# A four-layer decoder in one kernel: weights loaded in earlier stages, first steps without the weight preparation, output stored tile by tile, and a causal bias added in place

## The chip, the cores and the metric

The kernel runs on one core of one Trainium2 chip. A core has TensorE (PE), VectorE (DVE), ScalarE (ACT), GpSimd (POOL) and SyncE (SP), the last of which here only issues DMAs. The metric is the time of one execution in microseconds on the device, as the median of several runs.

## What is computed

A decoder of four layers over 128 sequences of 64 tokens with 128 features, all in float32. Each layer is an attention, a cross-attention to a second sequence `ctx_1024` and a feed-forward part, each followed by residual and LayerNorm:

```python
x = _layernorm(x + _L0_attn_ref(x, ...))               # 16 heads of 8, causal
x = _layernorm(x + _L0_xattn_ref(x, ctx, ctx, ...))    # 16 heads of 8
x = _layernorm(x + _L0_ffn_ref(x, ...))                # weights and tokens quantised
x = _layernorm(x + _L1_attn_ref(x, ...))               # linear attention
x = _layernorm(x + _L1_xattn_ref(x, ctx, ctx, mask, ...))
x = _layernorm(x + _L1_ffn_ref(x, ...))                # 8 experts, gated, routed
x = _layernorm(x + _L2_attn_ref(x, ...))               # recurrent, 4 inner layers
x = _layernorm(x + _L2_xattn_ref(x, ctx, ctx, lenS2, ...))
x = _layernorm(x + _L2_ffn_ref(x, ...))                # 8 experts, top 2
x = _layernorm(x + _L3_attn_ref(x, ...))               # 16 heads, relative bias
x = _layernorm(x + _L3_xattn_ref(x, ctx, ...))         # 8 heads of 64, own and ctx keys
x = _layernorm(x + _L3_ffn_ref(x, ...))                # 16 slots: gather, experts, combine
```

The softmax of the causal attention is what the last part of the change touches: scores of 64 queries by 64 keys per head plus a bias (0 or a large negative number), row maximum, subtract, exp.

## The kernel before

`x` and `ctx` stay in SBUF for the whole run, features on partitions: 128 x 8192. Twelve stages follow one another, each a function that opens a `Scope` with its own SBUF tiles, all of PSUM and its own semaphores, and a block with one program per engine. When a scope closes, its semaphores are cleared and all engines meet at a barrier (L42 to L45); the next stage then starts with its own DMAs on SP. A stage's first steps wait for all of its loads, then prepare its weights: DVE takes the mean of the output weight's rows out of it (so that LayerNorm's mean need not be subtracted later), PE multiplies it by the value bias into one output bias, DVE copies that to SBUF, and PE waits for it (`bo_ready`) before its first projection. The last stage is followed by a block in which SP stores `x` in four DMAs of 1 MB (L3386 to L3391).

Within a stage each engine's order is written out by `staggered(turns, period, (place, step), ...)` (L145): all steps of all tiles are sorted by tile times period plus place, and issued in that order; semaphores do the rest.

`mha` (L190) is used by four stages: causal (L0_attn), plain (L0_xattn), masked (L1_xattn) and relative (L3_attn). It has 32 tiles of 256 tokens. Per tile PE projects K and Q ("QK", L341, L342) and V (L349), computes scores in two halves of two PSUM banks each (S0, S1, L363), transposes the exponentials (T0, T1, L376), forms sums and outputs (ZO, L391, L398), projects out (y, L406, L408) and takes the variance (L413). Six of the eight PSUM banks form three pairs that go round: one serves S1(t), T0(t), S1(t+1); one QK and T1; one S0(t), V(t+1), S0(t+1). `wait_emptied` makes PE wait until the former user of a pair has been read (`emptied`). With a bias, DVE adds it to the scores from PSUM into the SBUF tile E (`add_bias`, L529), takes the row maximum (L550) and subtracts it (L560) within E; without a bias both read PSUM. Bank pairs of scores are thus free after the add with a bias, and after the subtract without. ACT takes exp, and DVE normalises (L569) and closes the tile (L583: scale and residual). The places of each variant stand in the table `PLACES`.

`quantised_ffn` (L0_ffn) first quantises its weights (ACT L765, DVE up to L869), and only then does PE turn the first tokens (L677), which DVE (L890) quantises. `linear_attention` (L1_attn, PE L1007, DVE L1147), `padded_attention` (L2_xattn, DVE L2344), `joint_attention` (L3_xattn, DVE L2648, PE L2497) and `slot_combine` (DVE L3281) begin alike. `routed_experts` (L1_ffn, L2_ffn) begins with a load of the router and DVE's copy of the identity beside it (L1517). It ends with 16 groups of 512 tokens: DVE and ACT weigh and mix the experts' rows (L1666, L1495), PE sums them with the residual (`gather_sum`, L1410, L1411), ACT squares (L1500), PE takes the variance (L1418), ACT forms the inverse root (L1506, L1508), DVE closes (L1672). The last stage's tiles are closed at L3333.

## Time and profile before

| | us |
|---|---|
| time, median of 3 runs | 4991.06 (4987.13 to 4992.86) |
| time of the profiled execution | 4995.66 |
| its span in the trace | 4993.9 |
| PE busy | 4483.5 (90%) |
| DVE busy | 3497.6 (70%) |
| ACT busy | 3088.7 (62%) |
| POOL busy | 1543.2 (31%) |

| stage | from | to |
|---|---|---|
| L0_attn (causal) | 5.8 | 334.6 |
| L0_xattn (plain) | 335.6 | 630.7 |
| L0_ffn | 631.7 | 942.7 |
| L1_attn | 943.6 | 1137 |
| L1_xattn (masked) | 1138 | 1445 |
| L1_ffn | 1446 | 1966 |
| L2_attn | 1967.8 | 3110 |
| L2_xattn | 3111.3 | 3191 |
| L2_ffn | 3192 | 3730.6 |
| L3_attn (relative) | 3731.7 | 4037.3 |
| L3_xattn | 4038.3 | 4633 |
| L3_ffn, last part (combine) | 4824.6 | 4980.3 |
| store | 4981.6 | 4993 |

The page divides the span into 40 slices, one digit of tenths per slice. The span is that of the instructions; the time of the execution is 1.8 us longer. The granted clock of PE is 0.955 of full speed over the span. The page:

```
PE   8989968798978997999999999679979989999887
DVE  8977767466865335989995999653349966666747
PEclk9999989898989998999999999889989999999989
DMA  2000000000021113000000000301130000000110
```

### The profile page before, as it was taken

The page shows a single profiled execution, that of the slowest core. Times are in us where ns is not written, and L with a number is a line of the kernel's source. Part 1 is how long each engine was busy: PE and PEld are TensorE (multiplying, and loading weights), DVE is VectorE, ACT ScalarE, POOL GpSimd, SP SyncE. Part 2 cuts the span into 40 slices and gives each one's busy share as a digit, 9 for nine tenths or more (in the row PEclk, how much of TensorE's full clock was granted, in tenths as well). Part 3 has the DMA queues.
Part 4 walks back from the last instruction along what each step waited for, and adds up shares of the span by engine and source line. Part 5 has one row for each costly group of instructions (what it writes and reads, how often), then busy time and mean ns, then how long its engine had stood idle before and what let it go on. Part 6 is the DMA issues. An engine that isn't in the chain of part 4 may idle for free. (4 is left out here: it accounts for less than half of the span.)

```text
span 4993.9 us, 101269 instructions
## 1 busy us (share of the span) xinstructions
PE 4483.5 (90%) x37623; PEld 2954.1 (59%) x37623; DVE 3497.6 (70%) x5384; ACT 3088.7 (62%) x5449; POOL 1543.2 (31%) x1948
## 2 busy tenths in 40 slices
PE   8989968798978997999999999679979989999887
PEld 6767746565757774444444443466656757777664
DVE  8977767466865335989999995653349966666747
ACT  5766667475665334888888887652247844444355
POOL 4434434213424771000000000037726622222326
PEclk9999989898989998999999999889989999999989
DMA  2000000000021113000000000301130000000110
GB/s 82 2 4 2 2 5 1 4 1 12 2 70 33 52 52 113 1 1 1 1 1 1 1 1 6 118 26 52 53 90 2 2 14 2 1 2 2 55 54 35
DMA packets 122746, 119.54 MB, mean 24 GB/s; under 512 B 19360, under 2 KB 104353, under 8 KB 120993
## 3 DMA queue, kind: packets, MB, share of 16 engines
q1 hardware_dynamic: 104864, 77.38, 5.0%
q0 software_dynamic: 17408, 35.69, 2.5%
q8 instruction: 317, 5.19, 0.4%
q14 instruction: 157, 1.28, 0.1%
HBM read 82.60 MB, written 30.41 MB: 23 GB/s over the span
## 5 line engine op out<-in xcount | busy, mean ns | idle before, releaser
L2242 POOL TENSOR_TENSOR L_xattn_E<-L_xattn_E,L_xattn_rz 128x256 f32<-128x256 f32 x16 | 10.2, 637 | 1276.7 <-DVE L_xattn_rz L2397 1276.7
L1335 POOL DMA_INDIRECT L_ffn_xg<-L_ffn_xrows,L_ffn_take x272 | 264.0, 971 | 317.5 <-DVE L_ffn_take L1619 235.3
L1395 PEld LDWEIGHTS L_ffn_ps<-L_ffn_down,L_ffn_mT 128*128 128x128 f32 x1904 | 247.5, 191 | 105.6 <-issue 79.3
L1341 POOL DMA_INDIRECT L_ffn_yrows<-L_ffn_yo,L_ffn_put x272 | 269.1, 989 | 94.5 <-issue 58.5
L1377 PE MATMUL L_ffn_ps<-L_ffn_up,L_ffn_xT 128*128 x544 | 258.6, 557 | 21.2 <-issue 9.2
L2483 POOL TENSOR_TENSOR L_xattn_E<-L_xattn_E,L_xattn_rz 128x1024 f32<-128x1024 f32 x64 | 123.9, 1935 | 477.8 <-DVE L_xattn_rz L2701 477.8
L1395 PE MATMUL L_ffn_ps<-L_ffn_down,L_ffn_mT 128*128 x1904 | 259.4, 276 | 2.5 <-DVE L_ffn_yo L1641 1.3
L1802 PE MATMUL L_attn_ps<-L_attn_mix,L_attn_wck 128*128 128x512 f32 x512 | 240.6, 592 | 0.0
L1818 PE MATMUL L_attn_ps<-L_attn_rl,L_attn_wcv 128*128 128x512 f32 x512 | 240.6, 592 | 0.0
L1478 ACT ACTIVATE L_ffn_mT<-L_ffn_ps 128x512 f32<-128x512 f32 x136 | 81.2, 597 | 237.9 <-PE L_ffn_ps L1386 237.9
L1630 DVE TENSOR_TENSOR L_ffn_m<-L_ffn_b,L_ffn_ps 128x512 f32<-128x512 f32 x136 | 93.6, 688 | 185.1 <-PE L_ffn_ps L1377 185.1
L301 POOL TENSOR_TENSOR L_attn_Kbd<-L_attn_Kt,main_head_of_row 128x1024 f32<-128x1024 f32 x64 | 147.9, 2311 | 242.7 <-issue 225.0
L1626 DVE TENSOR_TENSOR L_ffn_m<-L_ffn_sg,L_ffn_ps 128x352 f32<-128x352 f32 x136 | 70.9, 522 | 213.3 <-ACT L_ffn_sg L1468 213.3
L301 POOL TENSOR_TENSOR L_xattn_Kbd<-L_xattn_Kt,main_head_of_row 128x1024 f32<-128x1024 f32 x64 | 121.2, 1894 | 298.9 <-issue 277.3
L560 DVE TENSOR_TENSOR L_attn_E<-L_attn_E,L_attn_mx 128x1024 f32<-128x1024 f32 x128 | 210.8, 1647 | 2.3
L550 DVE TENSOR_REDUCE L_xattn_mx<-L_xattn_ps 128x16 f32<-128x1024 f32 x128 | 155.8, 1218 | 62.5 <-PE L_xattn_ps L363 62.3
L660 POOL TENSOR_SCALAR L_ffn_aq<-L_ffn_aq,L_ffn_qinv 128x512 f32<-128x512 f32 x64 | 127.0, 1999 | 171.5 <-ACT L_ffn_aq L808 171.5
L529 DVE TENSOR_TENSOR L_attn_E<-L_attn_ps,L_attn_bias 128x512 f32<-128x512 f32 x256 | 164.0, 681 | 22.8 <-PE L_attn_ps L363 19.6
L319 POOL COPY L_attn_Vz<-L_attn_Vt 64x64 f32<-64x64 f32 x512 | 168.3, 329 | 37.0 <-ACT L_attn_Vt L461 7.7
L1818 PEld LDWEIGHTS L_attn_ps<-L_attn_rl,L_attn_wcv 128*128 128x128 f32 x512 | 97.3, 190 | 122.5 <-issue 122.5
L1802 PEld LDWEIGHTS L_attn_ps<-L_attn_mix,L_attn_wck 128*128 128x128 f32 x512 | 92.6, 190 | 127.1 <-issue 92.8
L468 ACT ACTIVATE L_attn_E<-L_attn_E 128x1024 f32<-128x1024 f32 x128 | 134.8, 1053 | 47.8 <-DVE L_attn_E L560 47.7
(607 smaller groups left out, 13302.1 us busy)
## 6 DMA issues: line engine op xcount, KB each, us to landing
L_ffn_row_hot<-L_ffn_yrows SPq DMA_DIRECT2D x32, 256.0 KB, 2.9
L_ffn_col_hot<-L_ffn_yrows SPq DMA_DIRECT2D x32, 256.0 KB, 3.3
L_ffn_w<-in_L_ffn_e_W SPq DMA_DIRECT2D x32, 256.0 KB, 4.5
L_ffn_xrows<-L_ffn_xtok SPq DMA_DIRECT2D x42, 192.0 KB, 2.1
L_ffn_xg<-L_ffn_xrows,L_ffn_take POOLq DMA_INDIRECT x272, 2.5
L_ffn_yrows<-L_ffn_yo,L_ffn_put POOLq DMA_INDIRECT x272, 2.3
main_x<-in_xT SPq DMA_DIRECT2D x8, 512.0 KB, 7.6
main_ctx<-in_ctxT SPq DMA_DIRECT2D x4, 1024.0 KB, 11.5
```

The costliest lines, as they stand in the source:

```text
L301: pool.tensor_tensor(Kbd[u][:], Kt[u][:].rearrange("p (b o k) -> p b o k", b=NB, o=1).to_broadcast([P, NB, 4, S]), k["head_of_row"][:].rea ...
L319: z = pool.tensor_copy(Vz[u][64 * side:64 * side + 64, hp, b2:NB:2, :, c:c + 8], v[:, :, :, c:c + 8])
L468: act.activation(e, e, ACT.Exp).then_inc(exp_ready[half], 1)
L529: b = dve.tensor_tensor(E[t % 2][:, 8 * at:8 * at + 8, :].rearrange("p (a h) k -> p a (h k)", a=2), pair(f"S{half}", t)[:, g, :].rearrange ...
L550: dve.tensor_reduce(mx[t % 2][:, 16 * half:16 * half + 16], score_rows(half, t), AX, ALU.max) \
L560: dve.tensor_tensor(E[u][:, rows, :], score_rows(half, t), mx[u][:, rows].rearrange("p (a o) -> p a o", o=1).to_broadcast([P, 16, S]), ALU ...
L1335: pool.indirect_dma_start(xg[t % RING][:], None, xrows, bass.IndirectOffsetOnAxis(ap=take[:, t:t + 1], axis=0)) \
L1341: pool.indirect_dma_start(yrows, bass.IndirectOffsetOnAxis(ap=put[:, t:t + 1], axis=0), yo[t % RING][:], None).then_inc(scattered[t % RING ...
L1377: g = pe.matmul(ps[u][:, 0, 0:F], xT[u][:], up[:, bass.ds(at, F)], start=True, stop=True)
L1395: g = pe.matmul(ps[1][:, 3, 0:P], mT[u][0:rows[a], a * P:(a + 1) * P], down[0:rows[a], bass.ds(at + a * P, P)], start=(a == 0), stop=(a == ...
L1802: r = pe.matmul(ps[:, 5 + a % 2, :], wck[:, at(m)[0], a * P:(a + 1) * P], mix[:], start=True, stop=True)
L1818: r = pe.matmul(ps[:, 7, :], wcv[:, at(m)[0], a, :], rl[:, a, :], start=(a == 0), stop=(a == FT - 1))
```

## The change

**Weights early.** A new class `Early` holds tiles, one semaphore and their sources. The tiles of the next stages are allocated in an outer scope, and SP loads them in an earlier stage: those of L0_xattn, L0_ffn, L1_attn and L1_xattn (with its mask of 1 MB) in the first stage, behind x, the constants and ctx; those of L2_xattn in L2_attn; of L3_attn in L2_ffn; of L3_xattn (six of 256 KB) in L3_attn; of combine in the slots' expert stage. The routers are loaded in the first stage into tiles of the main scope, and DVE copies them. The lengths are laid out on 128 partitions on the host. Each `Early` is a scope, so eight further clears with barriers stand behind L1_xattn (four), L2_xattn (one), L3_xattn (two) and at the end (one).

```diff
+class Early:
+    def __init__(self, nc, ctx, name, **parts):
+        s = Scope(nc, ctx, name)
+        self.tile = {n: s.sb(n, shape, dt) for n, (shape, dt, _) in parts.items()}
+        self.source = {n: source for n, (_, _, source) in parts.items()}
+        self.loaded = s.sem("loaded")
+
+    def load(self, sp):
+        for n, source in self.source.items():
+            sp.dma_start(self.tile[n][:], source).then_inc(self.loaded, 16)
+
+    def wait(self, eng):
+        eng.wait_ge(self.loaded, 16 * len(self.tile))
...
                 for q, piece_loaded in enumerate(x_loaded):
                     c = slice(q * T // X_PIECES, (q + 1) * T // X_PIECES)
                     sp.dma_start(xres[:, c], d["xT"][:, c]).then_inc(piece_loaded, 16)
+                    if q == 0:
+                        sp.dma_start(bias_sb[:], bias).then_inc(bias_loaded, 16)
...
+                sp.wait_ge(rest_loaded, 16 * (len(LATER) + 4 + len(ROUTERS) + 1))
+            for stage in ahead:
+                stage.load(sp)
```

**First steps.** PE no longer waits for the prepared output weight or the output bias before its first tile. In `mha` the two bias products move to the first `outputs`, and DVE's copy to the first `normalise`:

```diff
-            pe.wait_ge(loaded, 16 * n_loads)
-            pe.wait_ge(weights, 1)
-            if has_wo:
-                pe.matmul(ps[:, 7, 0:1], W[3][:], column("bv"), start=True, stop=False)
-                pe.matmul(ps[:, 7, 0:1], k["center"][:], b_in[:], start=False, stop=True).then_inc(bo_mm, 1)
...
-            pe.wait_ge(bo_ready, 1)
+            wait_weights(pe)
+
+            def output_bias():
+                to = ps[:, 7, CT:CT + 1]
+                if has_wo:
+                    pe.wait_ge(weights, 1)
+                    pe.matmul(to, W[3][:], column("bv"), start=True, stop=False)
+                    pe.matmul(to, k["center"][:], b_in[:], start=False, stop=True).then_inc(bo_mm, 1)
...
             def outputs(t):
                 u = t % 2
+                if t == 0:
+                    output_bias()
...
             def normalise(t):
+                if t == 0:
+                    dve.wait_ge(bo_mm, 1)
+                    dve.tensor_copy(bo[:], ps[:, 7, CT:CT + 1]).then_inc(bo_ready, 1)
+                    dve.wait_ge(bo_ready, 1)
```

In `quantised_ffn` PE turns the first tokens, and DVE takes their range, before the weights are quantised; `w_ready` is waited for at the first expansion. In `linear_attention`, `padded_attention` and `joint_attention` the waits for the prepared weight move to the first `project_out`, while the one or two small bias products of PE stay in front.

PE's order at the head of L0_xattn, before (L330 and L331 are the bias products, L341 the K projection):

```order
L325 UNCONDITIONAL_BRANCH
L330 MATMUL L0_xattn_ps<-main_cols,L0_xattn_w3 128x1
L331 MATMUL L0_xattn_ps<-L0_xattn_b_in,main_center 128x1
L341 MATMUL L0_xattn_ps<-main_ctx,L0_xattn_w1 128x256
L342 MATMUL L0_xattn_ps<-main_x,L0_xattn_w0 128x256
```

and now (L375 is the K projection):

```order
L357 UNCONDITIONAL_BRANCH
L375 MATMUL L0_xattn_ps<-main_ctx,L0_xattn_early_w1 128x256
L376 MATMUL L0_xattn_ps<-main_x,L0_xattn_early_w0 128x256
L383 MATMUL L0_xattn_ps<-L0_xattn_early_w2,main_ctx 128x128 x2
L397 MATMUL L0_xattn_ps<-L0_xattn_Kbd0,L0_xattn_Qt0 64x256 x16
```

The two bias products have left the head; they come with the first `outputs`.

**The store.** The last block is gone. In `slot_combine` SP stores `x` in 16 pieces of 256 KB, each when its tile is closed:

```diff
+            for q in range(OUT_PIECES):
+                c = slice(q * T // OUT_PIECES, (q + 1) * T // OUT_PIECES)
+                sp.wait_ge(closed, (q + 1) * NT // OUT_PIECES)
+                sp.dma_start(out[:, c], k["x"][:, c]).then_inc(stored, 16)
+            sp.wait_ge(stored, 16 * OUT_PIECES)
...
-                for q in range(4):
-                    c4 = slice(q * T // 4, (q + 1) * T // 4)
-                    sp.dma_start(out[:, c4], k["x"][:, c4]).then_inc(stored, 16)
-                sp.wait_ge(stored, 64)
```

**The causal stage.** With `in_place=True` the bias is added to the scores where they lie in PSUM; maximum and subtract read PSUM, and the pair of banks is free after the subtract. The add no longer waits for the transposes of two tiles before. The places are new, the period of 9.2 is not:

```diff
-        scored = biased if bias is not None else sub_ready
+        scored = biased if bias is not None and not in_place else sub_ready
...
                     dve.wait_ge(s_mm[half], t + 1)
-                    if t >= 2:
+                    if t == 0:
+                        dve.wait_ge(bias_loaded, 16)
+                    if t >= 2 and not in_place:
                         dve.wait_ge(t_mm[half], t - 1)
...
+                        scores = pair(f"S{half}", t)[:, g, :].rearrange("p (a c) -> p a c", a=2)
                         b = dve.tensor_tensor(
-                            E[t % 2][:, 8 * at:8 * at + 8, :].rearrange("p (a h) k -> p a (h k)", a=2),
-                            pair(f"S{half}", t)[:, g, :].rearrange("p (a c) -> p a c", a=2),
+                            scores if in_place else E[t % 2][:, 8 * at:8 * at + 8, :].rearrange("p (a h) k -> p a (h k)", a=2),
+                            scores,
...
-            "QK": 0.0, "V": 1.0, "S0": 2.9, "bias0": 5.6, "max0": 9.5, "sub0": 9.6, "exp0": 11.6, "T0": 11.2,
...
+            "QK": 0.4, "V": 2.8, "S0": 3.6, "bias0": 4.3, "max0": 8.3, "sub0": 9.3, "exp0": 9.9, "T0": 13.6,
```

DVE's order for one tile in the causal stage, before (L529 add, L550 maximum, L560 subtract, L569 normalise, L583 close; two adds per half; the scope of this stage is L0_attn):

```order
L569 TENSOR_TENSOR L0_attn_On1<-L0_attn_ps,L0_attn_rz1 128x256 [waits L0_attn_y_mm,L0_attn_rz_ready]
L529 TENSOR_TENSOR L0_attn_E1<-L0_attn_ps,L0_attn_bias 128x512 [waits L0_attn_t_mm0,L0_attn_s_mm0]
L529 TENSOR_TENSOR L0_attn_E1<-L0_attn_ps,L0_attn_bias 128x512
L550 TENSOR_REDUCE L0_attn_mx1<-L0_attn_E1 128x16 [waits L0_attn_sub_ready0,L0_attn_biased0]
L560 TENSOR_TENSOR L0_attn_E1<-L0_attn_E1,L0_attn_mx1 128x1024 [waits L0_attn_t_mm0,L0_attn_max_ready0]
L529 TENSOR_TENSOR L0_attn_E1<-L0_attn_ps,L0_attn_bias 128x512 [waits L0_attn_t_mm1,L0_attn_s_mm1]
L529 TENSOR_TENSOR L0_attn_E1<-L0_attn_ps,L0_attn_bias 128x512
L550 TENSOR_REDUCE L0_attn_mx1<-L0_attn_E1 128x16 [waits L0_attn_sub_ready1,L0_attn_biased1]
L583 SCALAR_TENSOR_TENSOR main_x<-L0_attn_ps,L0_attn_bo,L0_attn_rs1 128x256 [waits L0_attn_rs_ready]
L560 TENSOR_TENSOR L0_attn_E1<-L0_attn_E1,L0_attn_mx1 128x1024 [waits L0_attn_t_mm1,L0_attn_max_ready1]
```

and now (L564 add, L585 maximum, L595 subtract, L608 normalise, L622 close):

```order
L564 TENSOR_TENSOR L0_attn_ps<-L0_attn_ps,L0_attn_bias 128x512 [waits L0_attn_s_mm0]
L564 TENSOR_TENSOR L0_attn_ps<-L0_attn_ps,L0_attn_bias 128x512
L608 TENSOR_TENSOR L0_attn_On1<-L0_attn_ps,L0_attn_rz1 128x256 [waits L0_attn_y_mm,L0_attn_rz_ready]
L585 TENSOR_REDUCE L0_attn_mx1<-L0_attn_ps 128x16 [waits L0_attn_sub_ready0,L0_attn_biased0]
L595 TENSOR_TENSOR L0_attn_E1<-L0_attn_ps,L0_attn_mx1 128x1024 [waits L0_attn_t_mm0,L0_attn_max_ready0]
L564 TENSOR_TENSOR L0_attn_ps<-L0_attn_ps,L0_attn_bias 128x512 [waits L0_attn_s_mm1]
L564 TENSOR_TENSOR L0_attn_ps<-L0_attn_ps,L0_attn_bias 128x512
L585 TENSOR_REDUCE L0_attn_mx1<-L0_attn_ps 128x16 [waits L0_attn_sub_ready1,L0_attn_biased1]
L564 TENSOR_TENSOR L0_attn_ps<-L0_attn_ps,L0_attn_bias 128x512 [waits L0_attn_s_mm0]
L564 TENSOR_TENSOR L0_attn_ps<-L0_attn_ps,L0_attn_bias 128x512
L595 TENSOR_TENSOR L0_attn_E1<-L0_attn_ps,L0_attn_mx1 128x1024 [waits L0_attn_t_mm1,L0_attn_max_ready1]
L622 SCALAR_TENSOR_TENSOR main_x<-L0_attn_ps,L0_attn_bo,L0_attn_rs1 128x256 [waits L0_attn_rs_ready]
```

The adds write PSUM and the subtracts read it; the first half's add of the next tile now comes before this tile's normalise and maximum, and here, as in about three of 32 tiles, the next tile's add0 (the last pair of L564) stands before the second half's subtract (L595).

**The end of the routed stages.** Three places are later: variance 4.0 to 5.5 (PE), inverse root 5.0 to 6.4 (ACT), close 6.6 to 8.0 (DVE), with the period of 2.7 unchanged.

```diff
-            staggered(NQ, 2.7, (1.4, gather_sum), (4.0, variance))
+            staggered(NQ, 2.7, (1.4, gather_sum), (5.5, variance))
...
-            staggered(NQ, 2.7, (0, weigh), (3.3, square), (5.0, rstd))
+            staggered(NQ, 2.7, (0, weigh), (3.3, square), (6.4, rstd))
...
-            staggered(NQ, 2.7, (0, mix), (6.6, close))
+            staggered(NQ, 2.7, (0, mix), (8.0, close))
```

PE's order in that tail, before (L1410 and L1411 sum a group, the groups 0 and 1 in ps0, 2 and 3 in ps1; L1418 is the variance of group 0):

```order
L1410 MATMUL L1_ffn_ps0<-main_x,main_center 128x128
L1411 MATMUL L1_ffn_ps0<-main_ident,L1_ffn_row_hot0 128x128
L1418 MATMUL L1_ffn_ps0<-L1_ffn_lg,main_avg 128x512
L1410 MATMUL L1_ffn_ps0<-main_x,main_center 128x128
L1411 MATMUL L1_ffn_ps0<-main_ident,L1_ffn_row_hot0 128x128
```

and now (L1435, L1436, and L1443):

```order
L1435 MATMUL L1_ffn_ps0<-main_x,main_center 128x128
L1436 MATMUL L1_ffn_ps0<-main_ident,L1_ffn_row_hot0 128x128
L1443 MATMUL L1_ffn_ps0<-L1_ffn_lg,main_avg 128x512
L1435 MATMUL L1_ffn_ps1<-main_x,main_center 128x128
L1436 MATMUL L1_ffn_ps1<-main_ident,L1_ffn_row_hot1 128x128
```

Behind the variance of group 0 came group 1; now it is group 2, so one more group lies between the sum and its variance.

## Rows read from the trace of the kernel before

**Rows 1.** Windows: stretch in us, length, busy us of each engine, PE clock, DMA share, GB/s.

```profile
20.00:325.00 305.00, 287.53 (x4408) 211.04 (x4409) 294.90 (x317) 215.29 (x372) 137.65 (x279) 0.98 0.05 19
1160.00:1440.00 280.00, 276.98 (x4484) 204.51 (x4482) 222.56 (x248) 175.72 (x310) 114.83 (x278) 0.99 0.01 2
```

**Rows 2.** Closes of the causal and the masked stage: count, ns, first and last start.

```profile
L583 DVE SCALAR_TENSOR_TENSOR main_x<-L_attn_ps,L_attn_bo,L_attn_rs x28: 474/475/476, 55.9 to 312.7; 128x256 f32<-128x256 f32 x28
...
L583 DVE SCALAR_TENSOR_TENSOR main_x<-L_xattn_ps,L_xattn_bo,L_xattn_rs x28: 477/477/477, 1185.6 to 1424.1; 128x256 f32<-128x256 f32 x28
```

**Rows 3.** Groups by form in 100:200 and 1200:1300: count, busy us, mean ns, idle before.

```profile
L560 DVE TENSOR_TENSOR L_attn_E<-L_attn_E,L_attn_mx 128x1024 f32<-128x1024 f32 x22 | 42.4, 1927 | 0.4
L529 DVE TENSOR_TENSOR L_attn_E<-L_attn_ps,L_attn_bias 128x512 f32<-128x512 f32 x42 | 26.9, 681 | 0.5 <-PE L_attn_ps L363 0.5
...
L550 DVE TENSOR_REDUCE L_attn_mx<-L_attn_E 128x16 f32<-128x1024 f32 x21 | 25.6, 1220 | 0.7
...
L560 DVE TENSOR_TENSOR L_xattn_E<-L_xattn_ps,L_xattn_mx 128x1024 f32<-128x1024 f32 x24 | 29.4, 1224 | 0.8
```

**Rows 4.** Timeline at the seams: start us, duration us, engine, line, operation, idle before.

```profile
11.64 0.15 DVE L502 TENSOR_SCALAR L_attn_bk<-main_cols 128x1 f32<-128x1 f32 x1 [11.64 <-DMA L_attn_bias<-in_const_causal]
...
334.14 0.48 DVE L583 SCALAR_TENSOR_TENSOR main_x<-L_attn_ps,L_attn_bo,L_attn_rs 128x256 f32<-128x256 f32 x1 [3.44 <-ACT L_attn_rs L263]
...
335.58 0.33 SPq L268 DMA_DIRECT2D L_xattn_w<-in_L_xattn_Wq  x1
...
340.89 1.20 PE L341 MATMUL L_xattn_ps<-main_ctx,L_xattn_w 128*128 128x256 f32 x2
...
635.60 0.63 ACT L765 ACTIVATE L_ffn_tmp<-L_ffn_w 128x512 f32<-128x512 f32 x1 [2.59 <-DMA L_ffn_conv<-in_L_ffn_conv]
...
642.54 0.69 PE L677 MATMUL L_ffn_ps<-main_ident,main_x 128*128 128x128 f32 x2 [4.83 <-DVE L_ffn_w L869]
...
646.45 0.68 DVE L890 TENSOR_SCALAR L_ffn_xq<-L_ffn_xq,L_ffn_qinv 128x128 f32<-128x128 f32 x3 [1.64 <-ACT L_ffn_xq L777]
...
948.58 0.15 DVE L1147 TENSOR_SCALAR L_attn_bq<-main_cols 128x1 f32<-128x1 f32 x1 [5.91 <-DMA L_attn_heads<-in_const_same_head]
...
1144.84 0.15 DVE L502 TENSOR_SCALAR L_xattn_bk<-main_cols 128x1 f32<-128x1 f32 x1 [7.79 <-DMA L_xattn_mask<-in_mask]
...
1147.08 1.20 PE L341 MATMUL L_xattn_ps<-main_ctx,L_xattn_w 128*128 128x256 f32 x2
...
3115.49 0.20 DVE L2344 CAST L_xattn_lengthf<-L_xattn_length 128x64 f32<-128x64 int32 x1 [5.32 <-DMA L_xattn_iota_k<-in_const_iota_k]
...
3195.01 0.23 DVE L1517 COPY L_ffn_wide<-main_ident 128x128 f32<-128x128 f32 x1 [3.85 <-DMA L_ffn_bg<-in_L_ffn_bg]
...
3736.64 0.15 DVE L502 TENSOR_SCALAR L_attn_bk<-main_cols 128x1 f32<-128x1 f32 x1 [6.03 <-DMA L_attn_bias<-in_L_attn_bias]
...
4045.88 0.69 DVE L2648 TENSOR_REDUCE L_xattn_wo_mean<-L_xattn_wo 128x4 f32<-128x512 f32 x1 [8.54 <-DMA L_xattn_wv<-in_L_xattn_Wv]
...
4047.71 0.77 PE L2497 MATMUL L_xattn_ps<-main_x,L_xattn_wk 128*128 128x256 f32 x1 [1.22 <-DVE L_xattn_bo L2655]
...
4829.32 0.15 DVE L3281 TENSOR_SCALAR L_combine_b_in<-main_cols 128x1 f32<-128x1 f32 x1 [5.51 <-DMA L_combine_diag<-in_const_half_rows]
```

**Rows 5.** Timeline at the end of the span; the page's row of a 256 KB load.

```profile
4979.58 0.69 DVE L3333 TENSOR_TENSOR main_x<-main_x,L_combine_rs 128x512 f32<-128x512 f32 x1 [2.66 <-ACT L_combine_rs L3272]
4981.63 3.08 SPq L3391 DMA_DIRECT2D yT<-main_x  x4
...
L_ffn_row_hot<-L_ffn_yrows SPq DMA_DIRECT2D x32, 256.0 KB, 2.9
```

**Rows 6.** Variance in the first routed stage's tail; timeline of one group there.

```profile
L1418 PEld LDWEIGHTS L_ffn_ps<-L_ffn_pr,main_avg x10: 186/188/189, 1912.4 to 1956.1; 128*128 128x128 f32 x10
...
1937.80 1.13 PE L1418 MATMUL L_ffn_ps<-L_ffn_eq,main_avg 128*128 128x512 f32 x2 [0.72 <-ACT L_ffn_eq L1500]
...
1941.00 1.14 DVE L1666 SCALAR_TENSOR_TENSOR L_ffn_row_hot<-L_ffn_col_hot,L_ffn_wt,L_ffn_row_hot 128x128 f32<-128x128 f32 x4 [1.50 <-ACT L_ffn_row_hot L1495]
```

321 lines of the change are left out of this document (162 added, 159 removed), and 6 rows, old and new, of the table PLACES.

## The prediction

> **What bounds the kernel now.** Read the page first by shares: PE is busy 90% of the span, but the 40 slices show it fall below 9 tenths around every change of stage and in two long stages, and DVE stand at 9 only in the first one and in the recurrent one. So the kernel is PE-bound inside most stages, and what is left lies at the seams, in the first stage and at the very end. I took these three in turn.
>
> The windows of two mha stages with the same PE work per tile [rows 1] show who sets the pace: in the causal stage DVE is busy 294.90 of 305 us (97%) and PE 287.53 (94%); in the masked one PE has 276.98 of 280 (99%) and DVE 222.56. The closes give the periods [rows 2]: (312.7−55.9)/27 = 9.51 us a tile with DVE as the bound, (1424.1−1185.6)/27 = 8.83 with PE. The groups of DVE by form [rows 3] tell why DVE is slow in the causal stage: its subtract, both inputs in SBUF, takes 1927 ns; the same subtract reading PSUM in the masked stage takes 1224. Two per tile.
>
> The first instructions of each stage [rows 4] show the seams. DVE's first operation waits in every stage for a DMA that was issued when the stage opened (bracket: idle time before it and its releaser), then come the weight's mean and the output bias, and only then does PE start on tile 0. The end of the span [rows 5] shows the store: nothing of it is issued before the last close has ended. At the end of a routed stage [rows 6] pe stands 0.72 us before each variance matmul for ACT's square.
>
> **The heads.** The change issues these loads one or more stages ahead and takes the preparation off PE's way to tile 0. From [rows 4], stage by stage; where the bracket counts from DVE's last operation of the stage before, I subtract the seam itself, which stays: 334.14+0.48 = 334.62 to 335.58, so 0.95, and up to 1.13 where DVE ended before the others.
> - L0_attn: loads are still its own; DVE's first operation came at 11.64, the bias being last in the queue. Now x's first piece comes ahead of the bias and the preparation (2.24 in L1_xattn) no longer stands before PE: 1.9, between 0 and 2.2.
> - L0_xattn: 335.58 to PE's first at 340.89: 5.3.
> - L0_ffn: the idle 2.59 for the load, and the token turn and quantise (642.54 to 646.45 = 3.91), which now runs beside the weights' quantisation: 6.5.
> - L1_attn: 5.91−0.95, plus 1.4 of preparation: estimated from L1_xattn's 2.24 below, less the small products that stay: 6.4.
> - L1_xattn: 7.79−0.95+(1147.08−1144.84 = 2.24) = 9.1.
> - L2_xattn: 5.32−1.13 = 4.2. L2_ffn: 3.85−0.9, less a 0.15 copy of the router: 2.8. L1_ffn has no such row; half of that, 1.4 (0 to 2.8).
> - L3_attn: 6.03−1.13, plus 1.0 for its preparation, shorter since it has no output weight: 5.9.
> - L3_xattn: 8.54−0.95+(4047.71−4045.88 = 1.83), less 0.6 for the small product that stays in front: 8.8.
> - combine: 5.51−0.8 = 4.7.
>
> Sum 57.0. The preparation does not vanish: it lies on DVE beside PE's first projections and scores, some 1 to 2 us in a tile where DVE has slack (masked: 222.56 of 280). If that cover fails, up to half of the heads comes back (a rival). The early DMAs cost nothing: they are issued by SP, which issues nothing else in those stages once its own loads are done, and the DMA engines are at 0.05 and 0.01 [rows 1]. In the first stage they queue behind x and the context.
>
> **The store.** Last close ends at 4979.58+0.69 = 4980.27, the span at 4993.9: 13.6. Sixteen pieces leave as their tiles close, so behind the last close stand one 256 KB piece, the barrier and the clears. A piece: 2.9 for a 256 KB load in the row of DMA issues, above a sixteenth of the whole store, (4993.9−4981.63)/16 = 0.8. I take 2.3, near the upper end, since one alone is mostly latency. With 1.9 for barriers and clears that leaves 4.2: saved 9.4 (8.8 to 10.9).
>
> **The new scopes.** Eight early scopes close: four behind L1_xattn, one behind L2_xattn, two behind L3_xattn, one at the end. Seam with one clear 0.95 [rows 4]; with two clears (block and outer scope at the end) 4980.27 to 4981.63 = 1.36 [rows 5]; so 0.43 each: −3.5.
>
> **The causal stage.** DVE's busy share is 294.90/305×9.51 = 9.19 a tile; the two subtracts give back 2×0.70 = 1.41, so 7.8. (Bounds: 0 if the subtract's length has another cause than its inputs; 1.41 by the masked row.) The max reads PSUM instead of SBUF. The add writes PSUM in place of SBUF, 681 ns now; no row has DVE writing PSUM. As nearest, reading it costs nothing: 1220 for a max from SBUF, 1224 for a subtract of as many elements from PSUM [rows 3]. I take 0 for it; the upper end is 0.07 for each of four.
>
> The Trainium skill, Perfetto Trace Analysis, section Optimizing Scalar/DVE Operations, says otherwise: an access overhead of about 60 ns for DVE on SBUF and about 125 on PSUM. By it the in-place add would cost 4×0.065 = 0.26 us more a tile. The rows contradict it for reads; for writes no run here shows it yet.
>
> What is new is who waits. The pair of score banks is free at the subtract and no longer at the add, so PE's next use of that pair (values of t+1, or the transposes T0) stands some 2.4 us later. Hence the new order: both halves run add, max, subtract in one go. At 7.8 plus the 0.3 that DVE idles per tile now, DVE's round is 8.1 to 8.4, below PE's. PE's own busy time is 287.53/305×9.51 = 8.97 here and 8.73 in the masked stage. I take a period of 8.97: 0.54×31 = 16.7. The rows of order show one flaw: in about 3 of 32 tiles add0(t+1) stands before sub1(t), so the subtract waits for a product of the next tile; 1.7 for them. Net 15. Bounds: 0 (period stays 9.5) and 21 (8.83, the masked one's).
>
> **The routed tails.** Two stages of 16 groups. In the first, one buffer of three comes back four times between 1912.4 and 1956.1, so a group takes 43.7/12 = 3.64 us [rows 6]. The variance now stands behind the next gather, so ACT's square is done by then, and the stall of 0.72 goes: at most 0.72×15×2 = 21.6. What is late next: close moves 1.4 later, and DVE's order (two mixes, close, mix) stays. So behind the variance come rstd (two ACT operations over 128x512, 0.63 each by L0_ffn's first in [rows 4]), the close (0.69 by that of [rows 5]), ACT's weighing (about 0.6, estimated) and DVE's mix of 1.14, for which DVE already idles 1.50; then the gather of a group further on. That is 3.7, about 4.0 with the handovers, and PE's own work of a group, 3.64−0.72 = 2.92, closes the ring, which spans two groups: (4.0+2.92)/2 = 3.46. Gain 0.1 to 0.2 a group: 3 a stage, 6 in all (0 to 21.6).
>
> **Sum.** 57.0+9.4−3.5+15+6 = 84. The profiled execution took 4995.66, its span 4993.9; 4995.66−84 = 4911.7. The profiled time stands 4.6 above the median of the runs, 4991.06, so **4907** by the median.
>
> **Rivals.** A measurement can tell about 0.2%, 10 us, from nothing.
> - *The loops gain nothing* (14%): the causal period stays 9.5 because PE now waits for the later subtract, and the routed tail trades one wait for another. Gain 62.9: 4928. For it: both orders are full of cross waits, 0.3 us of slack decides. Against: DVE has 97% and loses 1.4 of 9.2.
> - *Both reach PE's floor* (9%): 20+21 in place of 15+6: gain 104, 4887. For it: the masked stage does so with the same PE work.
> - *The heads are half given back* (8%): the preparation meets tile 0's own evictions on DVE, or PE runs at a lower granted clock behind a seam. Then 28 comes back: 4935.
> - *Writing PSUM is dearer* (4%): DVE's round of 8.4 gets 0.26 longer and reaches half-way into PE's; 0.14×28 = 4: 4911. This is what the skill's page would give; from the rows I hold its price for unlikely.
> - *The early loads come late* (1%): the first stage's SP waits for the context before it issues them, and a stage finds them unfinished. The heads give 0 and 27 is left: 4964. Against: 300 us lie between.
> - *Slower* (2%): holding the pair until the subtract serialises the causal loop: PE can't run ahead, and a tile costs DVE's 7.8 and half of PE's 8.8, 12.2 in all. That is 2.7×31 = 84 lost against 69 won elsewhere: 5006. It decides from a period of 9.5+69/31 = 11.7. Against: two further pairs of banks rotate beside it.
>
> **How the numbers follow.** The forecast's own chance is 62%; the predicted time is its time. Its band comes from the routed term (0 to 21.6), the causal term and the heads' small prices: some ±14. The range 4893 to 4931 takes it in with the second case's 4928, and leaves out the floor (9%), the half heads (8%) and the two rare cases (3%): 2 in 10. All but the last case are faster by more than 10 us: faster 0.97, same 0.01, slower 0.02.
>
> **What would show it.** Right: DVE's first operation of a stage no longer waits for a DMA, and PE's first one follows the seam within 0.1 to 1.5 us; the causal subtract at 1.22 us, adds at 0.68, closes 8.9 to 9.0 apart, PE at 98% and more; groups of the routed tail 3.4 to 3.5 apart with DVE's mix waited for by the gather; span end 4 us behind the last close. Wrong: a causal subtract still near 1.9 (then its inputs weren't the cause); adds at 0.75; PE idle before T0 or the values for sub_ready (the pair is held too long); first tiles that stretch as much as the heads shrank; a granted clock that falls where PE now starts earlier.

## The result and the profile after

The changed kernel takes 4903.26 us by the median of four runs (4899.31 to 4911.36), the kernel before 4991.96 in runs beside it: a ratio of 0.9826, with a 95% interval of 0.9809 to 0.9843. The forecast was 4907, with a range of 4893 to 4931. The page of the profiled execution:

```profile
span 4902.3 us, 101317 instructions
...
PE 4467.0 (91%) x37623; PEld 2943.4 (60%) x37623; DVE 3459.8 (71%) x5386; ACT 3088.7 (63%) x5449; POOL 1518.5 (31%) x1948
```

The span fell by 91.6 us (4993.9 to 4902.3), PE's busy time only by 16.5 (4483.5 to 4467.0): the other 75 us are idle time of PE that went. Two words are used below: a stage's opening is its first instruction, and the seam before it is the time from the last compute instruction of the stage before to that opening. Windows of the causal and the masked stage (as [rows 1]), then the causal closes, first all 32 and then the 18 from 149 us on (as [rows 2]):

```profile
20.00:305.00 285.00, 275.62 (x4327) 205.16 (x4331) 250.21 (x312) 212.32 (x365) 115.67 (x279) 0.98 0.09 29
1130.00:1400.00 270.00, 266.92 (x4320) 196.90 (x4312) 213.65 (x240) 170.66 (x304) 110.55 (x269) 1.00 0.01 2
```

```profile
L622 DVE SCALAR_TENSOR_TENSOR main_x<-L_attn_ps,L_attn_bo,L_attn_rs x32: 474/474/485, 43.0 to 320.5; 128x256 f32<-128x256 f32 x32
...
L622 DVE SCALAR_TENSOR_TENSOR main_x<-L_attn_ps,L_attn_bo,L_attn_rs x18: 474/474/483, 149.4 to 297.9; 128x256 f32<-128x256 f32 x18
```

PE is now the bound of the causal stage too: it is busy 275.62 of 285 us, 97%, and in the later part, from 149.4 to 298 us, all of the 148.6 us. The 18 later closes stand (297.9−149.4)/17 = 8.74 us apart. All 32 together need 277.5/31 = 8.95, so the early ones are slower; that comes back below. The groups by form between 100 and 200 us (as [rows 3]):

```profile
L564 DVE TENSOR_TENSOR L_attn_ps<-L_attn_ps,L_attn_bias 128x512 f32<-128x512 f32 x44 | 28.4, 692 | 9.2 <-PE L_attn_ps L397 9.2
L595 DVE TENSOR_TENSOR L_attn_E<-L_attn_ps,L_attn_mx 128x1024 f32<-128x1024 f32 x22 | 26.9, 1223 | 0.7
L585 DVE TENSOR_REDUCE L_attn_mx<-L_attn_ps 128x16 f32<-128x1024 f32 x22 | 26.8, 1220 | 0.4
```

The subtract takes 1223 ns in place of 1927, the maximum 1220 as before, the add into PSUM 692 in place of 681. The heads (as [rows 4]; the first row is the first stage, then close and K projection at the seam to L0_xattn, then PE and DVE at the opening of L1_xattn):

```profile
11.49 1.19 PE L375 MATMUL L_attn_ps<-main_x,L_attn_w 128*128 128x256 f32 x2 [11.49 <-DMA main_x<-in_xT]
...
320.51 0.48 DVE L622 SCALAR_TENSOR_TENSOR main_x<-L_attn_ps,L_attn_bo,L_attn_rs 128x256 f32<-128x256 f32 x1 [3.44 <-ACT L_attn_rs L288]
...
322.02 0.67 PE L375 MATMUL L_xattn_ps<-main_ctx,L_xattn_early_w 128*128 128x256 f32 x2 [2.50 <-PEq L45]
...
1104.23 1.19 PE L375 MATMUL L_xattn_ps<-main_ctx,L_xattn_early_w 128*128 128x256 f32 x2 [3.08 <-PEq L45]
...
1104.24 0.15 DVE L538 TENSOR_SCALAR L_xattn_bk<-main_cols 128x1 f32<-128x1 f32 x1 [0.98 <-PEq L45]
```

In the stages whose loads or first steps the change moved, PE starts within 0.1 us of the opening, on `PEq L45`, the barrier. Three places differ: in the first stage x's first piece releases PE, in the two routed stages PE waits 0.35 us for DVE's copy of the router, and in the gather before the slots' experts, which the change leaves as it was, PE still waits 4.4 us for a load (4561.86 against the opening at 4557.44; 4638.70 against 4634.30 before). In L0_ffn PE turns tokens at once, ACT starts on the weights at 1.3 us into the stage, and DVE quantises the first tokens at 8.1 us into it; before, it came at 14.75 (646.45 less 631.7):

```profile
613.74 0.63 PE L704 MATMUL L_ffn_ps<-main_ident,main_x 128*128 128x128 f32 x2
...
614.54 0.63 ACT L796 ACTIVATE L_ffn_tmp<-L_ffn_early_w 128x512 f32<-128x512 f32 x1
...
621.34 0.87 DVE L924 TENSOR_SCALAR L_ffn_xq<-L_ffn_xq,L_ffn_qinv 128x128 f32<-128x128 f32 x4
```

At the end (as [rows 5]) one store is left behind the last close, 4.4 us before the end of the span:

```profile
4897.20 0.69 DVE L3357 TENSOR_TENSOR main_x<-main_x,L_combine_rs 128x512 f32<-128x512 f32 x1 [2.66 <-ACT L_combine_rs L3296]
4897.93 0.33 SPq L3139 DMA_DIRECT2D yT<-main_x  x1
```

In the routed tail (as [rows 6]) the wait before the variance is gone. PE now waits in every second group for DVE's mix, and DVE for the root before a close:

```profile
1891.60 0.46 PE L1435 MATMUL L_ffn_ps<-main_x,main_center 128*128 128x128 f32 x2 [1.12 <-DVE L_ffn_row_hot L1691]
...
1895.90 0.69 DVE L1697 TENSOR_TENSOR main_x<-L_ffn_ps,L_ffn_both 128x512 f32<-128x512 f32 x1 [1.74 <-ACT L_ffn_both L1533]
```

Term by term, from the two traces (a stage's length runs from its opening to the next one's; each term is before less after; the measured heads, down to combine, sum to 55.2):

| term | forecast | measured | from |
|---|---|---|---|
| heads, L0_attn | 1.9 | 1.1 | first close, 46.7 to the 45.6 of e2, which has the old causal part |
| L0_xattn | 5.3 | 4.9 | stage length |
| L0_ffn | 6.5 | 6.4 | first close in the stage (57.1 to 50.7 us) |
| L1_attn | 6.4 | 6.4 | stage length |
| L1_xattn | 9.1 | 9.7 | opening to last close |
| L1_ffn, L2_ffn | 1.4, 2.8 | 1.4, 2.7 | last close to DVE's first operation, clears taken out |
| L2_xattn | 4.2 | 1.7 | opening to last close |
| L3_attn, L3_xattn | 5.9, 8.8 | 6.3, 10.3 | opening to last close |
| combine | 4.7 | 4.3 | opening to last close |
| store | 9.4 | 9.4 | last close's start to end, 14.3 and 5.1, a clear of 0.2 taken out |
| eight clears | −3.5 | −3.6 | the seams here less those of e10, which has none of them |
| causal stage, rest | 15 | 12.6 | first to last close 10.0 (287.5 to 277.5), first close 2.6 (45.6 to 43.0) |
| routed tails | 6 | 9.9 | 16 closes: 53.5 to 48.1, 52.6 to 48.1 |
| sum | 84 | 83.5 | |

The missing 8 us lie in stretches that the change does not touch: 3.7 in L2_ffn between its head and its tail, 2.5 in L0_ffn behind its first close, 1.4 in the experts' stage of L3_ffn, 0.6 in L2_attn. Such stretches vary between runs of identical code: L0_ffn takes 302 to 308 us in twelve traces, the experts' stage of L3_ffn 58.5 to 62, each with another granted clock (L0_ffn 302.1 us at 0.88 in the trace after, 307.3 at 0.86 in e2). The heads' terms have the same spread, as each stands on one pair of traces. From opening to last close L1_attn takes 187.0 us here and 184.5 in eight of the twelve (granted clock 0.96 and 0.97), which would make its term 8.9; L0_xattn takes 290.3 here and up to 293.9, which would make it 1.3; combine takes 151.4 or 149.2, a term of 4.3 or 6.5. So a single run says little about 5 us, and I read the experiments by stage.

### The profile page after: what moved, and what is told of

Same layout as the page of the kernel before. It is cut to its first block and busy times, and to the rows that moved or that the text cites. A ratio compares the mean times of both kernels' runs of the same rounds, so it can differ in the third digit from the quotient of the medians.

```text
span 4902.3 us, 101317 instructions
## 1 busy us (share of the span) xinstructions
PE 4467.0 (91%) x37623; PEld 2943.4 (60%) x37623; DVE 3459.8 (71%) x5386; ACT 3088.7 (63%) x5449; POOL 1518.5 (31%) x1948
## 5 line engine op out<-in xcount | busy, mean ns | idle before, releaser
L2263 POOL TENSOR_TENSOR L_xattn_E<-L_xattn_E,L_xattn_rz 128x256 f32<-128x256 f32 x16 | 10.2, 635 | 1268.4 <-DVE L_xattn_rz L2419 1268.4
L585 DVE TENSOR_REDUCE L_xattn_mx<-L_xattn_ps 128x16 f32<-128x1024 f32 x128 | 155.8, 1217 | 63.2 <-PE L_xattn_ps L397 63.2
L504 ACT ACTIVATE L_attn_E<-L_attn_E 128x1024 f32<-128x1024 f32 x128 | 134.8, 1053 | 46.7 <-DVE L_attn_E L595 46.7
L351 POOL COPY L_attn_Vz<-L_attn_Vt 64x64 f32<-64x64 f32 x512 | 146.5, 286 | 50.6 <-PE L_attn_ps L434 25.3
L595 DVE TENSOR_TENSOR L_xattn_E<-L_xattn_ps,L_xattn_mx 128x1024 f32<-128x1024 f32 x128 | 156.2, 1220 | 2.3
L1493 ACT ACTIVATE L_ffn_sg<-L_ffn_ps 128x352 f32<-128x352 f32 x136 | 63.0, 463 | 150.2 <-PE L_ffn_ps L1404 150.2
```

The lines of the kernel that those rows point to most:

```text
L351: z = pool.tensor_copy(Vz[u][64 * side:64 * side + 64, hp, b2:NB:2, :, c:c + 8], v[:, :, :, c:c + 8])
L504: act.activation(e, e, ACT.Exp).then_inc(exp_ready[half], 1)
L585: dve.tensor_reduce(mx[t % 2][:, 16 * half:16 * half + 16], score_rows(half, t), AX, ALU.max) \
L595: dve.tensor_tensor(E[u][:, rows, :], score_rows(half, t), mx[u][:, rows].rearrange("p (a o) -> p a o", o=1).to_broadcast([P, 16, S]), ALU ...
```

## The experiments

All start from the changed kernel; e11 goes on from e2, and e12 from e10. Their times are to be held against 4903.3. e1, e2, e10 and e12 have four or five runs each, the others one.

**e1_tie.** In the trace after, nine of the first steps between closes sum to 88.9 us. DVE around tile 6 (start us, duration, engine, line, operation):

```profile
65.56 1.29 DVE L564 TENSOR_TENSOR L_attn_ps<-L_attn_ps,L_attn_bias 128x512 f32<-128x512 f32 x2
...
66.88 1.22 DVE L585 TENSOR_REDUCE L_attn_mx<-L_attn_ps 128x16 f32<-128x1024 f32 x1
...
70.38 1.30 DVE L564 TENSOR_TENSOR L_attn_ps<-L_attn_ps,L_attn_bias 128x512 f32<-128x512 f32 x2 [2.28 <-PE L_attn_ps L397]
71.58 1.22 DVE L595 TENSOR_TENSOR L_attn_E<-L_attn_ps,L_attn_mx 128x1024 f32<-128x1024 f32 x1
72.72 0.48 DVE L622 SCALAR_TENSOR_TENSOR main_x<-L_attn_ps,L_attn_bo,L_attn_rs 128x256 f32<-128x256 f32 x1
...
74.64 0.43 DVE L608 TENSOR_TENSOR L_attn_On<-L_attn_ps,L_attn_rz 128x256 f32<-128x256 f32 x1 [1.45 <-ACT L_attn_rz L288]
```

The maximum of the second half (L585) ends at 68.1. What stands next is not its subtract but the add of the next tile (L564), which waits 2.28 us for PE's scores; the subtract (L595) comes at 71.58. Exp, transposes and outputs of that tile are all behind it, and the closes need four tiles to find their step again. PE waits 2.63 us for that subtract, and its granted clock falls behind it. Two windows of 10 us, one at each of the two places:

```profile
70.00:80.00 10.00, 7.37 (x52) 5.37 (x45) 6.93 (x10) 4.95 (x8) 1.56 (x7) 0.83 0.00 0
...
120.00:130.00 10.00, 7.66 (x56) 6.35 (x60) 7.60 (x10) 5.82 (x9) 1.92 (x5) 0.83 0.01 2
```

The edit:

```diff
-"S0": 3.6, "bias0": 4.3,
+"S0": 3.6, "bias0": 4.35,
```

> The changed kernel with bias0 at 4.35 in place of 4.3 in the causal stage, so that no tile has add0(t+1) ahead of sub1(t) on DVE. Theory (the ties): in the changed kernel's trace the closes stand 8.75 us apart, except for nine steps around the two tiles 6 and 11 that have the tie; these nine take 88.9 us where 9 x 8.75 = 78.8, so 10 us go. All steps become 8.75, the time 4893. Rival (something else between 60 and 130 us, such as the early loads or the clock of 0.83 in two windows, makes the long steps): the steps stay long, 4903.

4895.9 (median of four), and the closes:

```profile
L622 DVE SCALAR_TENSOR_TENSOR main_x<-L_attn_ps,L_attn_bo,L_attn_rs x32: 473/474/483, 41.5 to 309.0; 128x256 f32<-128x256 f32 x32
```

309.0−41.5 = 267.5 us from first to last, 10.0 less, and the granted clock in the same two windows is 1.00. The ties were the cause, and there were two of them (tiles 6 and 11), not three. A true tie does no harm: where the sums 9.2(t+1)+4.3 and 9.2t+13.5 are equal, the list has the subtract first. In these two tiles the first sum comes out as 59.49999999999999 against 59.5 and 105.49999999999999 against 105.5, by rounding, and the add goes first.

**e2_old_causal, e5_inplace_only, e6_places_only.** The causal part has two edits, taken apart here: the add in place, and the order.

```diff
-    masked), in_place=True)
+    masked), in_place=False)
```

is e6 (with `bias0` at 4.35); e5 puts the old row of PLACES back and keeps `in_place=True`; e2 does both.

> The changed kernel with the causal stage's bias added into SBUF again and with its old places; all else stays. Theory (in-place add and order carry the gain): closes 9.5 apart again, subtract at 1.93 us, first to last close 287 us in place of 277.5; time 4903 + 10 to 12 = 4913 to 4915. Rival (the stage's 13 us come from its head, the earlier first piece of x): first close early as now, 4903 to 4905.

> The changed kernel with the causal stage's old places, the add still in place. Theory (DVE's 1.4 us per tile is the bound, the order only fits it): subtract 1.22, period between 8.8 and 9.2, first to last close 273 to 285. Rival (the pair of banks held until the subtract serialises, and only the new places avoid it): period above 9.5, PE idle for sub_ready before S or V, stage longer than before the change.

> The changed kernel with the new places of the causal stage (bias0 4.35) but the bias added into SBUF. Theory: subtract 1.93 us, DVE busy 9.2 a tile, so it stays DVE-bound with 9.3 to 9.6 between closes. Rival (the order brings the gain, the subtract's length is hidden): 8.75 to 8.9.

Measured: e2 4916.2 (four runs), first to last close 287.4. e5 4941.1, with 10.1 us between closes and 305 from first to last. e6 4894.6, with 8.75 and 267.3. The subtract of e2 and the groups of e6 in the same stretch:

```profile
L595 DVE TENSOR_TENSOR L_attn_E<-L_attn_E,L_attn_mx 128x1024 f32<-128x1024 f32 x21 | 41.1, 1959 | 0.3
```

```profile
L595 DVE TENSOR_TENSOR L_attn_E<-L_attn_E,L_attn_mx 128x1024 f32<-128x1024 f32 x23 | 31.7, 1380 | 0.8
L564 DVE TENSOR_TENSOR L_attn_E<-L_attn_ps,L_attn_bias 128x512 f32<-128x512 f32 x46 | 29.5, 683 | 2.8 <-PE L_attn_ps L397 2.8
```

My theory of e6 was wrong. With the new order and the add still going to SBUF, the subtract takes 1380 ns, not 1930, and the stage is as fast as with the add in place. Its rival holds. And the add in place with the old order is what the slower rival of the prediction described. DVE waits for scores, PE's transposes for the subtract, each held up through the shared pair of banks (e5, idle times at the end of the rows, per 10 tiles):

```profile
L564 DVE TENSOR_TENSOR L_attn_ps<-L_attn_ps,L_attn_bias 128x512 f32<-128x512 f32 x40 | 25.8, 692 | 15.2 <-PE L_attn_ps L397 15.2
...
L410 PE MATMUL L_attn_ps<-main_ident,L_attn_E 128*128 128x128 f32 x157 | 20.7, 274 | 10.7 <-DVE L_attn_E L595 10.7
```

The row gives 10.7/10 = 1.1 us of PE per tile; DVE idles 1.5. That rival was priced at 12.2 a tile; it is 10.1, and it is the new places that avoid it. Even so e5, at 4941.1, is faster than the kernel before: the causal stage takes 17 us more than before, and the rest of the change gives more than that.

Why is the subtract short in e6? In the trace of before, its length has two sides. GpSimd at work beside it, and not (timeline of before, one tile):

```profile
151.05 1.89 POOL L301 TENSOR_TENSOR L_attn_Kbd<-L_attn_Kt,main_head_of_row 128x1024 f32<-128x1024 f32 x1 [4.51 <-issue]
151.32 2.70 DVE L560 TENSOR_TENSOR L_attn_E<-L_attn_E,L_attn_mx 128x1024 f32<-128x1024 f32 x1
...
156.84 1.22 DVE L560 TENSOR_TENSOR L_attn_E<-L_attn_E,L_attn_mx 128x1024 f32<-128x1024 f32 x1
```

At 151.32 GpSimd's multiply that spreads the keys (L301) has 1.62 us to go, and the subtract takes 2.70: those 1.62 and 1.08. At 156.84 GpSimd is free, and it takes 1.22. This holds for all 51 subtracts between 60 and 300 us of that trace: the 25 that start while L301 runs take the rest of it plus 1.08 us each, the 26 others 1.22 or 1.23. In e6 24 start beside the multiply, 23 of them 0.5 us before its end. These take 1.58 or 1.59, and the 24th 1.88, again the rest plus 1.08; the other 30 take 1.21 to 1.23. The Trainium skill (SBUF — State Buffer, section Who interferes with whom) has this rule: a VectorE operation with two SBUF inputs and a GpSimd operation that reads SBUF lock each other out, and the second to come waits for the whole of the first. The trace agrees, with 1.08 us behind the multiply's end in 49 of 49 (0.14 less than a subtract takes alone); and by the same rule an operation that takes one input from PSUM is free of it, as in e1, where 24 subtracts start beside the multiply and take 1.22 or 1.23.

**e11_pool_light** tests that directly, at the old order with the add into SBUF. From tile 2 on it leaves out three quarters of the spread of the keys and seven of the eight blocks of the spread of the values in the causal stage:

```diff
-                pool.tensor_tensor(
-                    Kbd[u][:],
+                n = 1 if name == "L0_attn" and t >= 2 else 4
+                pool.tensor_tensor(
+                    Kbd[u][:, :, 0:n, :],
...
+                            if name == "L0_attn" and t >= 2 and b2 + hp + side < 3:
+                                continue
```

> As e2_old_causal (old places, bias added into SBUF), but from tile 2 on GpSimd writes only a quarter of the spread keys and one of the eight blocks of the spread values in the causal stage, so the output is not the reference's; the rest is the same work. Theory (the subtract is long only while GpSimd works beside it; in the trace of before its length fits 1.22 + 0.58 x overlap in us): all subtracts at 1.22 to 1.6 us, period 8.8 to 9.1 with the old order, time about 4897 to 4903 against e2's 4916. Rival (it is long for its two SBUF inputs or for its place in the order): still 1.9 on average and 9.5.

```profile
L598 DVE TENSOR_TENSOR L_attn_E<-L_attn_E,L_attn_mx 128x1024 f32<-128x1024 f32 x22 | 26.8, 1220 | 0.4
```

All subtracts take 1.21 to 1.23 us: GpSimd was the cause of their length. The multiply is still there, at 0.61 us in place of 1.89, and 25 of the subtracts start beside its last 0.05 to 0.07 us; a rest as short as that doesn't show in them. But the closes only went from 9.5 to 9.05 (and to 9.05 and 9.47 in turn in the second half), 279.3 from first to last against 287.4 in e2 and 267.3 in e6. So of the 20 us between the old order (e2) and the new one (e6), at most 8 are the shorter subtracts; the other 12 are the order as such. The time, 4915.8, is near that of e2: of the 9.1 us that the causal stage is shorter, 7.5 came back in stages with the same code.

**e3b_tail_old** and **e4b_tail_mix**, the routed tails:

```diff
-            staggered(NQ, 2.7, (1.4, gather_sum), (5.5, variance))
+            staggered(NQ, 2.7, (1.4, gather_sum), (4.0, variance))
...
-            staggered(NQ, 2.7, (0, weigh), (3.3, square), (6.4, rstd))
+            staggered(NQ, 2.7, (0, weigh), (3.3, square), (5.0, rstd))
...
-            staggered(NQ, 2.7, (0, mix), (8.0, close))
+            staggered(NQ, 2.7, (0, mix), (6.6, close))
```

is e3b; e4b has 8.3 for `rstd` and 8.4 for `close` instead.

> The changed kernel with the three places of the routed tails as they were (4.0, 5.0, 6.6). Theory (the later variance brought the tails' gain): 16 closes take 53.5 and 52.6 us again in place of 48.1 twice, PE idle 0.72 before each variance; time 4903 + 10 = 4913. Rival (the tails are shorter for another reason, such as the loads' queue): still 48.1 and 4903.

> The changed kernel with the inverse root at 8.3 and the close at 8.4, so that DVE mixes group q+3 before it closes group q, and ACT weighs it before the root. Theory (the ring variance, root, close, mix, gather is what is left; PE waits 1.1 us for the mix in every second group): with the mix ahead of the close the ring is open and groups come every 2.9 us, PE's own work: 16 closes in 44, two stages, so 8 us less, 4895. Rival (the rows' loads with their ring of four buffers, or the gather's wait for an earlier close, hold it): the steps stay at 2.7 and 4.0, 4903.

e3b: the stall is back, and 16 closes take 52.7 and 54.0 us; the two stages are 3.6 and 6.6 us longer, 10.2 in all. The time of 4918.7 is 15 more, 5 of it in stages with unchanged code.

```profile
1893.54 1.13 PE L1443 MATMUL L_ffn_ps<-L_ffn_pr,main_avg 128*128 128x512 f32 x2 [0.72 <-ACT L_ffn_pr L1525]
```

e4b: 4889.6. The steps are 2.65 us each, 38.1 for 16 closes in both stages; the ring is open. Windows over the tail, after and e4b:

```profile
1864.00:1910.00 46.00, 39.33 (x251) 30.07 (x251) 28.49 (x90) 33.18 (x69) 0.00 (x0) 0.98 0.47 138
```

```profile
1875.00:1912.00 37.00, 36.35 (x240) 28.65 (x238) 28.19 (x87) 32.65 (x67) 0.00 (x0) 1.00 0.51 148
```

PE goes from 39.33 of 46 us to 36.35 of 37. I had expected 2.9 a group, the old step of 3.63 less the idle 0.72. But a stall costs more than the idle time that the profile shows. In the profile a product takes 0.28 us and the next one starts 0.11 behind it, so they overlap; before a stall there is no next one, and the whole 0.28 counts as busy; and the variance behind the stall is stretched. Without a stall the variance starts 0.23 us behind the last pair of sums:

```profile
1893.23 0.39 PE L1436 MATMUL L_ffn_ps<-main_ident,L_ffn_row_hot 128*128 128x128 f32 x2
...
1893.46 1.02 PE L1443 MATMUL L_ffn_ps<-L_ffn_eq,main_avg 128*128 128x512 f32 x2
```

In the trace of before that pair starts at 1936.69 and the variance at 1937.80, and it takes 1.13 us [rows 6]: 0.88 for the stall, and 0.1 for the stretched variance, which is the 0.98 between 3.63 and 2.65. The stages gain 9.5 and 9.9, the run 13.6.

**e7b_late_loads.** Every stage loads its own weights when it opens (the routers alone stay early); the first steps stay lazy.

```diff
-            for stage in ahead:
-                stage.load(sp)
...
+            if early is not None:
+                early.load(sp)
```

> The changed kernel with every stage's weights loaded in that stage again, while the first steps stay as changed (PE's first tile doesn't wait for the prepared weight). Theory (of the 57 us of the heads, DMA waits are the larger part): the idle times before the change come back less the seam, 3.6, 3.9, 5.0, 6.9, 4.2, 3.5, 7.6 and 4.7 in the eight stages, 39 in all: 4942. Rival (the preparation in front of PE was the larger part, the loads were hidden in barrier and table load): 13 to 18 more, 4916 to 4921.

4948.4, 45 more. By stages: 3.7, 5.8, 5.6, 7.8, 3.3, 2.8, 7.7 and 4.2, which is 40.9 against the 39 expected. By its first close L0_ffn's 5.8 is 3.0 (50.7 to 53.7), and the sum 38. The loads are the larger part of the heads.

**e9_eager.** The loads stay early, but the four mha stages prepare their output bias before PE's tile 0 again.

```diff
             wait_weights(pe)
...
+            output_bias()
+            pe.wait_ge(bo_ready, 1)
...
+            dve.wait_ge(bo_mm, 1)
+            dve.tensor_copy(bo[:], ps[:, 7, CT:CT + 1]).then_inc(bo_ready, 1)
```

> The changed kernel with the output bias prepared in front again in the four mha stages: PE multiplies it first and waits for DVE's copy before tile 0. The loads stay early. Theory (what PE waits for in front is lost, as the sum assumed): 1.9, 1.7, 2.2 and 1.0 us in the four stages, 6.8 in all, first closes later by that: 4910. Rival (the preparation is given back behind the head anyway, since DVE does the same work before its first add or maximum): first closes where they are, 4903 to 4905.

4913.95. The opening of L0_xattn:

```profile
320.40 0.15 DVE L539 TENSOR_SCALAR L_xattn_bk<-main_cols 128x1 f32<-128x1 f32 x1 [1.03 <-PEq L45]
...
322.77 1.22 PE L378 MATMUL L_xattn_ps<-main_ctx,L_xattn_early_w 128*128 128x256 f32 x2 [0.25 <-DVE L_xattn_bo L556]
```

PE's first projection comes 2.4 us behind the opening in place of 0.0. From opening to first close L0_xattn takes 2.7 us more and L1_xattn 2.3, near what the sum assumed. In L0_attn and L3_attn the first close comes 0.7 earlier, not later: no cost of the preparation in front shows there (in L0_attn x's first piece only lands at 11.49; in L3_attn there is no output weight to centre). In traces of the same code the first close of L0_attn spreads from 42.0 to 45.0 us and that of L0_xattn from 38.0 to 40.8 us behind the opening (40.7 in e9), that of L1_xattn only from 29.0 to 29.9 (31.5 in e9). So L1_xattn's 2.3 stands by its close, and L0_xattn's rather by the 2.4 of its first projection. The lazy preparation is worth about 5 us in the four mha stages, where 6.8 was expected, and the rest of the run's difference lies in untouched ones. What the lazy first steps give in L0_ffn, L1_attn, L3_xattn and combine no run separates.

**e8b_store_block.** The output stored in four DMAs behind the last stage.

> The changed kernel with the output stored by four DMAs in a block behind the last stage, as before. Theory (the pieces leave while later tiles are computed and cost nothing there): from the last close to the end of the span 5.1 us now, 14.1 then (before the change 14.3, less or more a clear), time 4912; the last stage's own length unchanged. Rival (the stores slow the combine stage, so leaving them out gives some of it back): combine stage shorter by over 1 us and the time under 4911.

```profile
4893.27 0.69 DVE L3353 TENSOR_TENSOR main_x<-main_x,L_combine_rs 128x512 f32<-128x512 f32 x1 [2.66 <-ACT L_combine_rs L3292]
4895.86 3.09 SPq L3429 DMA_DIRECT2D yT<-main_x  x4
```

4909.9. From the end of the last close, 4893.96, to the end of the span, 4908.1, it is 14.1 us in place of 4.4: 9.7 more, a little over the 9 expected. Likely, though no run separates it, the seam before the store costs more with the clear of combine's early weights in it (in the kernel before, without that clear, the whole is 13.6). The combine stage itself took 149.1, 2.3 less than after, and the time is under 4911, which is what the rival said; but e1 and e4b, with the stores in it, have 149.2 too, so the stores cost it nothing.

**e10_best, e12_best_sbuf.** e1's place, e4b's tails, and the semaphores of `Early` in the main scope, so that the eight clears and barriers go; e12 has `in_place=False` besides.

```diff
-        s = Scope(nc, ctx, name)
-        self.tile = {n: s.sb(n, shape, dt) for n, (shape, dt, _) in parts.items()}
+        self.tile = {n: ctx.enter_context(nc.sbuf_tensor(f"{name}_{n}", shape, dt)) for n, (shape, dt, _) in parts.items()}
...
-        self.loaded = s.sem("loaded")
+        self.loaded = Early.main.sem(name + "_loaded")
```

> The changed kernel with bias0 at 4.35, the tails' root and close at 8.3 and 8.4, and the semaphores of the early loads kept in the main scope, so that the eight extra clears with their barriers go. From the runs so far: 10 for the ties, 20 for the two tails (38.1 in place of 48.1 us for 16 closes), 8 x 0.43 to 0.57 = 4 for the seams: 4903 - 34 = 4869. Rival (the clears cost nothing, and the tails' gain is partly given back, as e4 with 13.6 shows): 4876 to 4880.

> As e10_best, but the causal bias is added into SBUF as before the change. Theory (the order carries the gain and keeps GpSimd away from most subtracts; PE is the bound): same as e10_best within 2 us. Rival (the add in place is worth something beside GpSimd): 5 to 20 us slower than e10_best.

e10 4875.63 (4871.63 to 4880.74), ratio to before 0.9758 (0.9744 to 0.9772); e12 4875.56 (4873.32 to 4878.92), ratio 0.9762 (0.9748 to 0.9776). Both beat the changed kernel by 28 us. The seam behind L1_xattn, last close to opening, shrinks from 3.1 to 1.2 us with four clears less, that behind L3_xattn from 2.1 to 1.0 with two. The expectation of 4869 was 7 too low; its rival's 4876 is met, though for the wrong reason: the clears did give 3.6 and the tails 19 to 20, but other stretches came out longer (in e10 the last two steps between closes of the causal stage by 3 against e1, L0_ffn by 3 against the trace after). Between the two kernels there is nothing that five runs each can tell: the add in place brings no measurable time once the order is right.

## Why the prediction was right, and where it was not

- **The frame held.** PE-bound stages, time at the seams, in the first stage and at the end; that is where 83.5 of the 91.6 us came from. That the time came within 4 us of the forecast is partly luck: no term has the other 8, and errors in the terms cancel (the step between the causal closes was forecast 5.0 too high and L2_xattn 2.5, the tails 3.9 too low and L3_xattn 1.5).
- **The heads.** 57.0 forecast, 55.2 measured by the table. The step "idle before DVE's first operation less the seam, plus the preparation" gives most stages within 1 us. L1_ffn's 1.4 was a guess, half of another stage's, and it hit. L0_attn was over-priced, as the first close moved 1.1 for 2.1 of PE's first projection (13.61 to 11.49). L3_xattn gave 10.3 for 8.8, though its first close moved 8.3. L2_xattn is the one clear miss, 1.7 for 4.2, and there the rival of the half heads came true: PE starts earlier at the lower granted clock. Two windows of 10 us from the opening, before, after, and in e2 (same code as after in this stage):

```profile
3111.30:3121.30 10.00, 3.64 (x51) 3.37 (x52) 5.26 (x18) 1.69 (x2) 0.61 (x1) 0.54 0.26 72
3121.30:3131.30 10.00, 9.24 (x73) 6.39 (x73) 5.53 (x15) 3.32 (x10) 1.23 (x2) 0.60 0.26 74
```

```profile
3062.20:3072.20 10.00, 7.26 (x85) 6.27 (x85) 7.66 (x24) 3.04 (x6) 1.22 (x2) 0.50 0.29 86
3072.20:3082.20 10.00, 10.00 (x60) 5.84 (x60) 3.96 (x10) 3.71 (x9) 0.61 (x1) 0.54 0.26 75
```

```profile
3076.70:3086.70 10.00, 6.72 (x85) 5.73 (x85) 7.66 (x24) 3.04 (x6) 1.22 (x2) 0.54 0.30 86
3086.70:3096.70 10.00, 9.98 (x77) 6.32 (x78) 6.09 (x16) 5.16 (x13) 1.15 (x2) 0.78 0.26 74
```

PE worked 3.64 of the first 10 us before and 7.26 after, but the granted clock stays near half, 1.2 of 2.4 GHz, through most of the 20 us in both (0.54 and 0.60 before, 0.50 and 0.54 after), behind a seam at which PE had been idle. The second close of the stage came 7.09 us behind the first in place of 4.55: 2.5 of the 4.2 given back. In e2 the clock rises earlier (0.78 in the second window), the step is 4.88 and the stage 2.2 us shorter, so 4.0 of the 4.2 are won. Of the twelve traces with this stage's code three are of that kind (75.8 or 75.9 us from opening to last close), eight of the other (78.0 to 78.3), and one lies between. So that part depends on when the clock rises, in which runs of equal code differ.
- **The store and the clears.** 9.4 and −3.5 forecast, 9.4 and −3.6 measured. The clears are not equal: the four behind L1_xattn cost 1.9, the two behind L3_xattn 1.1, the one behind L2_xattn 0.4 and the one at the end 0.2.
- **The causal stage.** The term that was mis-sized is "I take a period of 8.97 ... 1.7 for them". The 8.97 was PE's busy time in a stage where it waits for DVE; where it does not wait the steady period is 8.74, near the 8.73 of PE's work in the masked stage, so 20 us and not 16.7 were there (e1, 287.5 to 267.4). And the two ties cost 5 us each, 10 in all, for two reasons. An exp, the transposes and the outputs stand behind a delayed subtract, and not just the 0.7 us of its own wait. And the clock falls to 0.83 in the window: in e3b, where it did not fall at the second tie, the stage takes 276.4 from first to last close for 277.5, so that part is about 1 us of the 5. Two errors of opposite sign left 10.0 between the closes for 15. The table's other 2.6 is an earlier first close, which no step of the forecast has, and which is less than the spread of 42.0 to 45.0 us that it has in equal code.
- **The reason for it.** "Its subtract, both inputs in SBUF, takes 1927 ns; the same subtract reading PSUM takes 1224" was read as a price of the inputs. It is a price of the neighbour: with two SBUF inputs it waits for GpSimd's multiply to end. The forecast's bound "0 if the subtract's length has another cause than its inputs" was too coarse, since the order took most of it away with the inputs unchanged (1380 ns in e6), and with it the same 20 us.
- **The slower rival** was real as a mechanism: in place with the old order costs 10.1 us a tile, and the new places alone kept it off. It would not have made the kernel slower: the rival itself needed 11.7 for that, and e5 stays at 4941.1.
- **The rule of dearer PSUM** (the Trainium skill, Perfetto Trace Analysis, section Optimizing Scalar/DVE Operations) was weighed at 0.065 us per add; the add from and to PSUM takes 11 ns more (692 for 681), the maximum nothing (1220 for 1220). The measurement decides for the rows.
- **The routed tails.** 6 forecast, 9.9 measured. The ring was right, and its waits stand in the rows; mis-sized was PE's part, 2.92, of which PE's own products are 2.65 (e4b). With that the forecast's own sum gives (4.0+2.65)/2 = 3.33 in place of 3.46, and 3.35 came, as 2.70 and 4.00 in turn. The upper bound of 21.6 was too low for the same reason: with the ring open e4b gains 15.4 and 14.5 on the kernel before, 29.9. It is the error of the 8.97 again: PE's busy time, taken where it stalls, is more than its own work.

## What to carry to other kernels

A wait for loads at a stage's opening can be added up from the idle time before the first operation of each stage, and moving the loads a stage ahead returns nearly all of it; count on less where the engine then starts at the lower clock. When an operation is slower in one stage than in another, compare its shortest and longest instance and look at what runs beside them before blaming its operands: a mean hides two lengths. Don't take an engine's busy time beside stalls for its floor: here 8.97 was 8.74, and 2.92 was 2.65. In an order made by sorting sums of floating-point places, two steps with equal sums can change sides in single tiles by rounding, so look for ties one by one and keep places apart; each tie costs as much as the chain behind the delayed step, not just its own wait. And a table of one trace before and one after hides a spread: stages of the same code differed by 2 to 5 us here with the granted clock.

## What the runs showed of the hardware

- A subtract of 128x1024 with both inputs in SBUF takes 1.22 us when GpSimd is free at its start. When GpSimd's multiply is under way it takes what is left of the multiply plus 1.08 us (up to 2.74), in 49 of 49 cases with 0.3 us or more left. I had read the mean of 1.93 as one length. It goes the other way too: in e2 a GpSimd copy (L351) of 0.23 us takes 1.01 when it starts beside such a subtract, ten times between 60 and 160 us.
- Behind a seam the granted clock stayed near half for most of the first 20 us of L2_xattn, before (0.54, 0.60) and after (0.50, 0.54), though PE's busy time in the first 10 went from 3.64 to 7.26. In most traces work that is moved forward there is done at half the clock.
- An add of 128x512 that reads and writes PSUM takes 692 ns, one that reads PSUM and writes SBUF 681 to 683.
- A stall of PE costs more than its idle time in the profile: 0.98 us a group in the routed tail, where 0.72 stand in the row.
- While PE waited at the two ties of the causal stage (busy 7.37 and 7.66 of 10 us), its granted clock in the window fell to 0.83; without the ties it stayed at 1.00.
